# Attention and expert block: the norms' last step on another engine, head pairs, one bias product and a new order of the first turns

## The reference

```
x = x + attention(layernorm(x), ctx)      # 16 heads of 16, bias -slope_h * |k - q - (Nk - Nq)|
g = softmax(layernorm(x) @ Wg + bg)       # top 2 of 8, weights made to sum to 1
x = x + sum over the two experts e of  w_e * (gelu(layernorm(x) @ W1[e] + b1[e]) @ W2[e] + b2[e])
```

## Time and profile before

| | us |
|---|---|
| median of three runs | 503.34 |
| lowest, highest | 501.44, 504.68 |
| the profiled execution | 508.91 |
| its span | 507.1 |
| PE busy in the span | 419.6 |
| DVE busy | 312.6 |
| ACT busy | 232.4 |
| POOL busy | 223.7 |

### The profile page before, as it was taken

One profiled execution on the slowest core, in us unless ns is written; L12 is line 12 of the kernel. 1 busy time (PEld: TensorE's weight loads), 2 busy tenths in 40 slices (PEclk: granted clock), 3 DMA queues, 4 the chain that ended last, 5 costly groups with the idle time before them and its releaser, 6 DMA issues. The chain is left out here.

```text
span 507.1 us, 16158 instructions
## 1 busy us (share of the span) xinstructions
PE 419.6 (83%) x5137; PEld 330.3 (65%) x5138; DVE 312.6 (62%) x875; ACT 232.4 (46%) x607; POOL 223.7 (44%) x305
## 2 busy tenths in 40 slices
PE   5565768897888999995179899989989998999981
PEld 2554556676666778873168677668867876777760
DVE  5357848796778777554526466636664765566560
ACT  1333636564555564563234444534543553445430
POOL 3123528887888886677602222222222232122232
PEclk9865979898989999998579999989998999999997
DMA  6574455555646535333322223113222322122110
GB/s 225 134 229 150 139 152 189 175 175 192 215 136 185 165 123 163 122 123 127 127 64 37 39 41 53 35 29 45 46 44 31 53 38 43 34 43 47 22 12 0
DMA packets 52967, 50.70 MB, mean 100 GB/s; under 512 B 22672, under 2 KB 47024, under 8 KB 52784
## 3 DMA queue, kind: packets, MB, share of 16 engines
q1 hardware_dynamic: 45192, 41.07, 27.0%
q0 software_dynamic: 7152, 8.47, 9.9%
q10 hardware_dynamic: 576, 0.53, 0.3%
HBM read 33.73 MB, written 17.50 MB: 101 GB/s over the span
## 5 line engine op out<-in xcount | busy, mean ns | idle before, releaser
L976 PE MATMUL ps<-area,wts 128*128 128x128 f16 (+1 forms) x2896 | 197.0, 243 | 0.1
L976 PEld LDWEIGHTS ps<-area,wts 128*128 (+1 forms) x2896 | 157.5, 103 | 41.0 <-issue 2.1
L976 PE MATMUL ps<-wts,area 128*128 x624 | 153.4, 330 | 2.2 <-DVE area L934 1.8
L718 ACT ACTIVATE area<-ps,late 128x128 f32<-128x128 f32 x312 | 89.2, 368 | 115.0 <-PE ps L976 115.0
L932 DVE TENSOR_SCALAR area<-area 128x512 f16<-128x512 f32 x78 | 33.0, 424 | 77.8 <-ACT area L718 77.7
L976 PE MATMUL ps<-area 128*128 128x154 f16 (+2 forms) x928 | 71.0, 236 | 12.0 <-DMA area<-qd 11.1
L976 PEld LDWEIGHTS ps<-area 128*128 128x128 f16 (+1 forms) x928 | 59.8, 107 | 21.2 <-issue 8.1
L595 POOL DMA_INDIRECT out<-o,row_id x20 | 31.6, 1579 | 95.1 <-issue 65.0
L595 POOL DMA_INDIRECT out<-xn,row_id x19 | 30.0, 1579 | 92.4 <-issue 79.8
L804 DVE TENSOR_REDUCE mx<-ps 128x3 f32<-128x462 f32 (+1 forms) x96 | 53.1, 579 | 24.3 <-PE ps L976 23.9
L621 ACT ACTIVATE area<-ps 128x512 f32<-128x512 f32 x80 | 47.3, 595 | 27.7 <-PE ps L976 25.5
(11 more groups left out here) (121 smaller groups left out, 419.1 us busy)
## 6 DMA issues: line engine op xcount, KB each, us to landing
stage<-in_w SPq DMA_DIRECT2D x32, 512.0 KB, 5.0
area<-xlist SPq DMA_DIRECT2D x39, 130.0 KB, 2.0
area<-qd SPq DMA_DIRECT2D x16, 256.0 KB, 2.7
qd<-wts SPq DMA_DIRECT2D x48, 64.0 KB, 1.9
area<-in_x SPq DMA_DIRECT2D x16, 128.0 KB, 2.3
out<-area SPq DMA_DIRECT2D x16, 128.0 KB, 1.8
xlist<-pad_rows SPq DMA_DIRECT2D x11, 130.0 KB, 2.5
area<-in_b SPq DMA_DIRECT2D x1, 1024.0 KB, 5.0
```

What stands on the lines that cost most here:

```text
L718: last = nc.scalar.activation(h32[par][:, c * P:(c + 1) * P], h_ps[par][m][:, f * P:(f + 1) * P], ACT.Gelu_apprx_tanh, bias=b1T[:, ds(e * ...
L976: return nc.tensor.matmul(out_, lhsT, rhs, start=start, stop=stop, skip_group_check=skip)
```

## The change

Six edits, in words; the diff below is cut to their core.

1. POOL no longer normalises. Behind the power it computes one number per row, -mean * rstd, and ACT computes x * rstd + that number over 128x256. For the second norm this is the first thing ACT does in the next turn; for the first norm it stands behind the last exponentials, and in turns before -1 behind the query.
2. A group of scores takes its heads in pairs: where both heads of a pair lie in one group, one product of 314 columns makes them. The groups are now 3, 3, 2, 3, 3 and 2 heads, in the heads' natural order.
3. The bias row's two halves stand on two partitions, so that one product adds both.
4. The keys are made, split, written and read by batch: batch 0 first, then the query of tile 0, then batch 1. The first load brings only the key weights and batch 0's context. ACT issues the transfers of the keys' bias rows.
5. In turns before 0, DVE takes the statistics of the first norm ahead of the maxima, and PE and DVE make the query ahead of the scores and their maxima.
6. In the last two turns DVE splits expert weights at the end of its turn.

```
-GROUPS = [(0, 3), (3, 3), (6, 3), (9, 3), (12, 2), (14, 2)]
+GROUPS = [(0, 3), (3, 3), (6, 2), (8, 3), (11, 3), (14, 2)]
...
             def rstd(t, mv, rs, ready, done, shifted):
                 pool.wait_ge(ready, t + 1)
                 pool.tensor_tensor(rs[:, 1:2], rs[:, 0:1], c32[:, C_HALF:C_HALF + 1], ALU.pow).then_inc(done, 1)
+                pool.wait_ge(done, t + 1)
+                pool.tensor_scalar(rs[:, 2:3], mv[:, 0:1], rs[:, 1:2], -1.0, ALU.mult, ALU.mult).then_inc(shifted, 1)
...
-                pool.tensor_scalar(xn, xr[:, t % 8, :], mv1[:, 0:1], rs1[:, 1:2], ALU.subtract, ALU.mult).then_inc(s.xn_d, 1)
-                pool.tensor_scalar(xn2[:], xr[:, t % 8, :], mv2[:, 0:1], rs2[:, 1:2], ALU.subtract, ALU.mult).then_inc(s.xn2_d, 1)
...
+            def normed2(t):
+                act.wait_ge(s.shift2, t + 1)
+                wait(act, s.x2T_ps, t)
+                wait(act, s.xs_lo, t)
+                nc.scalar.activation(xn2[:], xr[:, t % 8, :], ACT.Identity, bias=rs2[:, 2:3], scale=rs2[:, 1:2]).then_inc(s.xn2_d, 1)
+                act.wait_ge(s.xn2_d, t + 1)
...
             for b in range(B):
+                sp.wait_ge(s.k_hi, b + 1)
+                for a in (0, 1):
+                    sp.dma_start(parts[:, a, :, b], k16[:, b, 0]).then_inc(S[f"kd_w{b}"], 16)
+                sp.wait_ge(s.k_lo, b + 1)
+                sp.dma_start(parts[:, 2, :, b], k16[:, b, 1]).then_inc(S[f"kd_w{b}"], 16)
+                if b == 0:
+                    write_q(0)
...
+                if i < 0 and f1 is not None and f1 > 0:
+                    norm1(f1)
-                if sc is not None:
+                if sc is not None and i >= 0:
                     for g in range(3):
                         maxima(sc, g)
                 if f2 is not None and f2 > 0:
                     query_lo(f2)
+                if sc is not None and i < 0:
+                    for g in range(3):
+                        maxima(sc, g)
...
-                for j in range(n):
-                    hh, p = (first + j) // NP, (first + j) % NP
-                    dst = ps[:, seq % 3, j * KW:j * KW + NK]
-                    last = mm(dst, qs[:, slot, p, :], kk[:, b, p, hh * KW:hh * KW + NK], True, kink is None, True)
+                while at_ < end:
+                    p, hh = at_ // 2, at_ % 2
+                    both = hh == 0 and at_ + 1 < end
+                    width = KW + NK if both else NK
+                    dst = bank[:, (at_ - first) * KW:(at_ - first) * KW + width]
+                    last = mm(dst, qs[:, slot, p, :], kk[:, b, p, hh * KW:hh * KW + width], True, kink is None, True)
...
+                    at_ += 1 + both
...
                 if f2 is not None and f2 > 0:
                     turn_normed(f2)
+                    if i < 0:
+                        query(f2)
...
-                    for z in range(2):
-                        last = mm(misc[:, D:2 * D], c16[0:1, H_SMALL:H_SMALL + P], bo_hl[:, z, :], False, z == 1)
-                    last.then_inc(s.pr_ps, 1)
+                    mm(misc[:, D:2 * D], c16[0:2, H_SMALL:H_SMALL + P], bo_hl[:], False, True).then_inc(s.pr_ps, 1)
```

More of the change, by code:

```diff
@@ L642, in turn @@
                 units = weight_units(i)
+                if b2 is not None:
+                    normed2(b2)
                 if f2 is not None and f2 > 0:
-                    normed(f2)
+                    turned(f2)
                 if b1 is not None:
@@ L650, in turn @@
                     query(f2)
+                if i < -1 and f1 is not None and f1 > 0:
+                    normed1(f1)
                 if b2 is not None:
@@ L677, in turn, with normed1, turned @@
                     exps(mt, 4)
+                if i >= -1 and f1 is not None:
+                    normed1(f1)
                 for u in units[1:2]:
                     split_w_hi(u)
-            def normed(t):
+            def normed1(t):
+                act.wait_ge(s.shift1, t + 1)
+                wait(act, s.xnT_ps, t)
+                nc.scalar.activation(xn, xr[:, t % 8, :], ACT.Identity, bias=rs1[:, 2:3], scale=rs1[:, 1:2]).then_inc(s.xn_d, 1)
+            def normed2(t):
[4 more added lines that the diff above has]
+                act.wait_ge(s.xn2_d, t + 1)
+            def turned(t):
                 act.wait_ge(s.xnT_ps, t + 1)
@@ L690, in query @@
                 nc.scalar.activation(q16[:, t % 2, 0, :], q_ps[:, D:2 * D], ACT.Copy, scale=SQ).then_inc(s.q_hi, 1)
-            normed(0)
-            act.wait_ge(s.k32_d, 2)
-            nc.scalar.copy(k16[:, 0], k32).then_inc(s.k_hi, 1)
-            act.wait_ge(s.kb_d, 2)
-            nc.scalar.copy(kb16[:, 0], kb32).then_inc(s.kb_hi, 1)
-            query(0)
+            normed1(0)
+            turned(0)
+            for b in range(B):
+                act.wait_ge(s.k32_d, 2 * (b + 1))
+                nc.scalar.copy(k16[:, b, 0], k32[:, b]).then_inc(s.k_hi, 1)
+                act.wait_ge(s.kb_d, b + 1)
+                nc.scalar.copy(kb16[:, b, 0], kb32[:, b]).then_inc(s.kb_hi, 1)
+                if b == 0:
+                    query(0)
+                act.wait_ge(s.kb_lo, b + 1)
+                for hh in range(2):
+                    act.dma_start(kd[hh, R_BIAS:R_MAX, :, b].rearrange("a n k -> n a k"), kb16[hh * NP:(hh + 1) * NP, b]).then_inc(S[f"kd_w{b}"], 16)
             for i in range(FIRST, LAST):
@@ L842, in turn @@
                     maxima(sc, 3)
-                if f1 is not None and f1 > 0:
+                if i >= 0 and f1 is not None:
                     norm1(f1)
-                for u in earlier[1:2]:
+                for u in earlier[1:2] if i < NT else []:
                     split_w_lo(u)
@@ L848, in turn @@
                     maxima(sc, 4)
-                for u in units[0:1]:
+                for u in units[0:1] if i < NT else []:
                     split_w_lo(u)
@@ L873, in turn @@
                     dve.transpose(nbT[:, sc % 2, :], nb16[:]).then_inc(s.nbT_d, 1)
+                for u in earlier[1:2] + units[0:1] if i >= NT else []:
+                    split_w_lo(u)
                 if i == -3:
@@ L1036, in scores @@
                 first, n = GROUPS[g]
-                for j in range(n):
-                    hh, p = (first + j) // NP, (first + j) % NP
-                    dst = ps[:, seq % 3, j * KW:j * KW + NK]
-                    last = mm(dst, qs[:, slot, p, :], kk[:, b, p, hh * KW:hh * KW + NK], True, kink is None, True)
+                end, bank = first + n, ps[:, seq % 3, :]
+                at_ = first
+                while at_ < end:
[4 more added lines that the diff above has]
+                    last = mm(dst, qs[:, slot, p, :], kk[:, b, p, hh * KW:hh * KW + width], True, kink is None, True)
                     if kink is not None:
                         keys = kinks[:, kink * N_KEYS:kink * N_KEYS + NK]
-                        for m in ((0, 1), (2,))[hh]:
-                            last = mm(dst, diagonal(p, m), keys, False, m > 0, True)
+                        for h in range(at_, at_ + 1 + both):
+                            dst = bank[:, (h - first) * KW:(h - first) * KW + NK]
+                            for m in ((0, 1), (2,))[h % 2]:
+                                last = mm(dst, diagonal(p, m), keys, False, m > 0, True)
+                    at_ += 1 + both
                 last.then_inc(s.s_ps, 1)
@@ L1095, in turn @@
                         scores(sc, g)
-                if f2 is not None and f2 > 0:
+                if f2 is not None and f2 > 0 and i >= 0:
                     query(f2)
```

149 lines of the change are left out of this document (75 added, 74 removed).

## The result

The changed kernel takes 510.34 us (median of four runs, 509.64 to 511.98), the kernel before 503.98 in four runs beside it: 1.014 times as long, 95% interval 1.0095 to 1.0185. Measured again in a later group it was 1.0114 (1.0089 to 1.0139). The prediction said 491 us and held 510 for a case of 6 in 100. It was wrong, and in sign. Disturbed runs are left out of all ratios: of the kernel with the norms alone that took away at least four of twelve, and of the one with the first norm alone on ACT the run that was profiled.

What follows compares the result with a forecast made beforehand. PE's waits in the first 247 us, for POOL's second norm and SP's DRAM round trips, were taken as the bound; 3.2 + 1.4 + 2.5 + 4.0 + 1.2 = 12.3 us took the median 503.3 to 491 us, range 484 to 501.

Steps and rivals of the forecast that it cites:

- Second norm: Six turns, 128 to 199 us: last step on ACT gains 0.6 us in four, 0.4 in two; 3.2 us (0 to 6.6).
- First norm: End of ACT's turn: the pass fits ACT's room; 0, with 0.5 us gain or at most 0.4 loss per turn.
- Pairs: Score products: weight loads hide under products, so a pair takes as long as two single ones; 0, within 0.1 us a turn.
- Rival B: Score products: weight loads count after all, so pairs save 5.8 us more, giving 485 us; chance 0.08.
- Bias product: One bias product for two saves 0.16 us in each of nine turns where PE is the limit; 1.4 us (0 to 2.5).
- Last four turns: Turns without query: second norm on ACT saves 0.58 us each, 2.3 us; with the weight residue 2.5 us (1.5 to 3.5).
- Adds 0 to 0.9: Last turns: the weight residue moved behind the second norm's variance gains 0 to 0.9 us; 0.2 taken.
- The start: First turns: keys by batch and query ahead of scores bring scores and first maxima sooner; 4 us (0 to 7).
- the chain behind them is unchanged: Start: from the first maxima to the third tile's scores remains 12.2 us, since SP's order is the same.
- Early turns: 54 to 128 us: second norm's 0.6 us mostly behind SP's chain; 1.2 us over six turns (-2 to 4).
- C: Head of ACT's turn: new pass waits for POOL's shift and blocks the query's copy; transposes 1.0 us later, 510 us; chance 0.06.
- A: SP's queue: its chain of DRAM round trips hides the gain in early and middle turns; 499 us; chance 0.19.

Runs made afterwards that it cites:

- the norms alone: Kernel before with only both norms' last step moved to ACT, the second's pass at the head of ACT's turn: 1.0014, and 1.012 when measured again.
- The idle products: Changed kernel with 12 unread fp16 products on PE ahead of the query product in each turn: 0.9992 of the kernel before, 505.4 us.
- all but the norms: Changed kernel with both norms' last step back on POOL, everything else as changed: 0.9975 of the kernel before.
- the second norm alone: Kernel before with only the second norm's last step on ACT, at the head of its turn, first norm on POOL: 1.0391, 523.4 us.
- the later pass: Changed kernel with the second norm's ACT pass moved behind the copies of transposed first norm and attention output: 0.978 of the kernel before, 499.8 us.

## Why the prediction was wrong

The list in its own order.

1. Second norm: forecast a gain of 3.2 us; the step costs. With the first norm on ACT either way, the second norm's step takes the kernel from 0.9875 to 1.0114 (two groups), 2.4%, some 12 us; with the first on POOL 3.9%. The chain of this point (power, shift, ACT, copy, query, transposes) is the right one, and the trace shows it link by link. Three of its terms failed. The pass was priced by the cast of its size, 0.41 us, and takes 0.60. "The gate weights end some 2 us sooner, at about the time of the variance" was the worst: the removed 2.27 us became not 0.19 but 1.22 to 1.32 in every turn from 60 to 190 us, POOL's shift beside DVE's residue (1.31 in the turn shown), so the power starts 0.61 us after the variance, not 0.05. Together with 0.1 us more between links and a last step that came 0.2 sooner, that makes 3.61 us for 2.93. And the sum had no term for the clock: the wait of 1.7 to 1.9 us was moved to stand ahead of the eight fp32 products, which then ran at 1.2 GHz in four of ten turns, 0.9 us each, with the products behind them. The idle products gave 6.8 us back, with a clock above that of the kernel before too. One sum was wrong as well: without a backlog in the turn of the earlier trace rows POOL's pass would have ended at 129.85 and the transposes come near 129.9, against 130.85, so the new order loses 0.9 there and not 0.3. At equal backlog this turn loses that much either way, and the whole gain hung on the backlog getting shorter by more; it went from 1.6 to 0.6 us. A forecast of 2.93 us against a break-even of 3.54, from three prices taken off neighbours, deserved more than 6 in 100 for the other side.

2. First norm: forecast 0, "with 0.5 us of gain in the turns where PE waited". It gained 0.5%, 2.6 us, alone, and 1.0% in the changed kernel (0.9875 with it, 0.9975 with both norms on POOL, two groups): a term put at nothing.

3. Pairs: forecast 0; right for the pairs by themselves, 1.0015 with the bias product. The rule of the Trainium skill that was weighed against it (TensorE: Matmul & The Clock Gate, Back-to-back issue gap) would have given 5.5 us, 1.1%, outside that interval; with the prediction's own 84 and 105 ns it is 0.38 us a turn and 6.0 us, not 0.35 and 5.5. Rival B falls.

4. Bias product: forecast 1.4 us. The product and the next scores stand 0.21 us apart, for 0.32 for the two before:

```profile
136.07 0.28 PE L1004 MATMUL ps<-bo_hl,c 2*128 2x256 f16 x1
136.28 0.53 PE L1004 MATMUL ps<-area 128*128 128x314 f16 x5
```

That is 0.11 us a turn instead of 0.16, about 1 us, too small to be seen in 1.0015.

5. Last four turns: forecast 2.5 us, got none. The transposes come 1.69 to 1.76 us after the variance for 2.02, 0.3 us a turn instead of 0.58, but 2.60 for 2.07 in the last, where the moved weight residue runs beside POOL's power. "Adds 0 to 0.9" had the wrong sign. No run took this edit back alone.

6. The start: forecast 4 us. A lead of 4.9 us was there at 75 us of the span in the profiled pair, though not by the way I gave. The first scores came at 23.89 us, not at 22.8, the third tile's gained 0.4 us only, the turn at 54 us started 1.4 us sooner, and 3.5 us came in the two turns behind it. The step "the chain behind them is unchanged" failed, since the maxima's write met the loads sooner. By the end it is not there: all but the norms is worth 0.25%. The rule of the Trainium skill on transfers under 512 bytes (DMA: Bandwidth & Descriptors, Specifications) changed nothing that these runs could single out.

7. Early turns: forecast 1.2 us of gain, with "query copied 1 us later where SP waits for it" as the bound of -2. In the profiled pair they lost 1.8 us: 3.5 gained up to the turn of tile 6, 5.2 lost from there to 128 us.

Of the rivals, C is what happened, by its place. That its figure (510) came true is in part luck: it priced the chain at 4.53 us from variance to transposes with POOL's backlog at 1.6 us. That is what the second norm alone shows at full clock (4.59 to 4.61); the changed kernel, with the backlog at 0.6, has 3.61 in six turns, over C's line of 3.54 by 0.07, and 4.5 in the four where the clock fell, of which C said nothing. A is true beside it: in three kernels where PE's wait for the norm was cut without harm (0.9949, 0.9973, 0.9875) PE's wait for the queries' read rose from 5.8 to between 10.6 and 11.0 us, and SP's read of the maxima moved out of the way gives 1.1% in the kernel before, and from 0.978 to 0.967 with the later pass. I had rejected it because PE waited for no query from 128 us on; but it was the norm's wait that covered SP's.

## What to carry to other kernels

An instruction that waits belongs behind everything in its queue that is ready and that somebody waits for; when it is put at the head, add to its price the whole chain behind it, and compare with the wait of the place where it was. Look at what the engine does right after a wait: the fp32 products behind a wait took 2.08 us for 1.16 where the clock fell, so put the wait behind them. When a wait is taken away, look for the wait it covered: here a small DRAM round trip in a queue in order, and the change with one instruction moved on ACT and one on SP is 3.3% faster than the kernel it began from.

## What the runs showed of the hardware

POOL's operations on one element per partition are not of constant price: beside a DVE weight residue of 128x1024 the shift took 1.31 us for 0.27 and the power 1.47 for 0.55 (changed kernel, 136.02 and 241.83 us). ACT's pass of 128x256 with scale and bias per row takes 0.60 us, where its copy takes 0.37 and its cast 0.41. The Trainium skill has a price for the one and names the other, and I had used neither. In the Trainium skill ScalarE: Activation LUTs (What ACT_TABLE_LOAD costs) gives an activation with immediate operands 186 ns and 0.833 ns an element, and 93 ns more for each operand that is a pointer to one value per partition: an estimate by that page is 0.40 us for the cast and 0.585 for a pass with two such operands; the trace agrees with both (0.41 and 0.60). In the Trainium skill GPSIMD Engine Reference (Specifications) names the contention of POOL with DVE instructions that have two inputs in SBUF, as the weight residue has; the two rows agree with it, and no run here moved the residue alone. Twelve idle fp16 products in a wait of up to 1.9 us took the granted clock from 0.88 and 0.91 to 0.95 and 1.00 and more than paid for themselves: 6.8 us less than the changed kernel.
